# Splits of a cross-network kernel in two groups, half steps as float32r parts, one more z buffer

## The reference

```python
z0 = einsum('bid,bjd->bdij', x0, x0)          # 39 x 39 products, symmetric
cur0 = relu(z0 @ W0)                          # 1521 -> 128
next_h, direct0 = split(cur0, 2)              # 64 and 64
z1 = einsum('bid,bjd->bdij', x0, next_h)      # 39 x 64 products
cur1 = relu(z1 @ W1)                          # 2496 -> 128
z = sum([direct0, cur1], over d)              # 192 values a sample
h = relu(concat(z, dense_ctx) @ W_top1 + b_top1)
y = relu(h @ W_top2 + b_top2) @ W_top3
```

## Time and profile before

| | |
|---|---|
| median of 3 runs | 1515.13 us (1511.45 to 1517.09) |
| the profiled execution | 1511.94 us, its span 1510.1 us |
| PE (TensorE matmuls) busy | 1434.6 us (95%) |
| VectorE (DVE) busy | 1393.3 us (92%) |
| GpSimd (POOL) busy | 939.0 us (62%) |
| ScalarE (ACT) busy | 825.2 us (55%) |
| DMA | 293.08 MB, mean 194 GB/s |

### The profile page before, as it was taken

The page is one execution under the profiler, slowest core; times in us unless marked ns, Lnnn a source line. Parts: engine busy times, 40 slices in busy tenths (PEclk is TensorE's granted clock), DMA queues, the critical chain, the costliest instruction groups (busy, mean ns, idle before and its releaser), DMA issues.

```text
span 1510.1 us, 15015 instructions
## 1 busy us (share of the span) xinstructions
PE 1434.6 (95%) x4458; PEld 794.5 (53%) x4458; DVE 1393.3 (92%) x1253; ACT 825.2 (55%) x897; POOL 939.0 (62%) x604
## 2 busy tenths in 40 slices
PE   3179999999999999999999999999999999999999
PEld 2145555555555555555555555555555555555556
DVE  2179999999999999999999999999999999999993
ACT  0155555655655555655655555655655555655555
POOL 7638888868687786868687786868687780000000
PEclk7589999999999999999999999999999999999999
DMA  5069989999989899999989999899998998898510
GB/s 150 6 160 203 227 216 218 206 220 212 221 198 222 206 217 214 208 223 201 220 203 216 214 212 220 208 213 203 212 216 223 212 210 216 204 222 207 170 35 1
DMA packets 137289, 293.08 MB, mean 194 GB/s; under 512 B 37646, under 2 KB 62878, under 8 KB 137080
## 3 DMA queue, kind: packets, MB, share of 16 engines
q1 hardware_dynamic: 102642, 278.48, 77.2%
q0 software_dynamic: 19200, 4.95, 2.9%
q10 hardware_dynamic: 15366, 8.70, 2.1%
HBM read 284.08 MB, written 7.87 MB: 193 GB/s over the span
## 4 chain that ended last, share of the span: by engine, by line
PE 90%; DVE 4%; issue 2%; another core or an unknown queue 2%; ACT 0%; DMA 0%; DVEq 0%; SPq 0%
PE psB L493 42%; PE psA L493 14%; PE psB L511 7%; PE psB L514 6%; PE psB L518 6%; PE psA L501 2%; PE psA L511 2%; PE psA L514 2%; PE psA L518 2%; PE psB L501 2%; DVE z L902 1%; PE psA L485 1%; DVE z_lo L911 1%; DVE z_split L902 1%
## 5 line engine op out<-in xcount | busy, mean ns | idle before, releaser
L472 POOL DMA_INDIRECT emb<-in_tbl,ids_all x600 | 938.8, 1565 | 309.7 <-issue 178.9
L493 PE MATMUL psB<-z,w 128*128 128x512 f32 x1544 | 690.1, 593 | 5.3 <-DVE z L902 5.3
L767 ACT ACTIVATE z_hi<-z_split 128x1024 fp32r<-128x1024 f32 (+1 forms) x286 | 301.4, 1057 | 464.9 <-DVE z_split L902 372.4
L493 PEld LDWEIGHTS psB<-z,w 128*128 128x128 f32 x1544 | 292.4, 190 | 362.7 <-issue 346.0
L902 DVE TENSOR_TENSOR z<-h_quad,x_lay 128x1024 f32<-128x1024 f32 x354 | 420.5, 1218 | 7.4 <-PE psB L493 5.4
L911 DVE TENSOR_TENSOR z_lo<-z_split,z_hi 128x1024 fp32r<-128x1024 f32 (+1 forms) x286 | 349.3, 1221 | 6.3 <-ACT z_hi L767 3.2
L902 DVE TENSOR_TENSOR z_split<-h_quad,x_lay 128x1024 f32<-128x1024 f32 x222 | 268.4, 1221 | 0.0
L720 ACT ACTIVATE h_quad<-psA 32x1024 f32<-32x1024 f32 x248 | 251.7, 1015 | 6.1 <-DVE feat_side L987 2.4
L493 PE MATMUL psA<-z,w 126*128 126x512 f32 x512 | 241.9, 594 | 0.0
L511 PE MATMUL psB<-z_hi,w_hi 128*128 128x512 f32 x444 | 157.7, 436 | 0.0
L493 PEld LDWEIGHTS psA<-z,w 126*128 126x128 f32 x512 | 97.3, 190 | 98.4 <-issue 92.7
(11 more groups left out here) (113 smaller groups left out, 862.5 us busy)
## 6 DMA issues: line engine op xcount, KB each, us to landing
x_lay<-x_rows SPq DMA_DIRECT2D x1152, 128.0 KB
x_more<-x_rows SPq DMA_DIRECT2D x62, 504.0 KB
bases<-x_rows SPq DMA_DIRECT2D x62, 468.0 KB
x_lay<-x_rows SPq DMA_DIRECT2D x64, 256.0 KB
x_ring<-x_rows SPq DMA_DIRECT2D x31, 504.0 KB
emb<-in_tbl,ids_all POOLq DMA_INDIRECT x600
x_last<-x_rows SPq DMA_DIRECT2D x64, 128.0 KB
x_rows<-x_side ACTq DMA_DIRECT2D x58, 120.0 KB
```

What stands on the lines that cost most here:

```text
L472: nc.gpsimd.indirect_dma_start(emb[t % 2][:, f * D:(f + 1) * D], None, tables[f], bass.IndirectOffsetOnAxis(ids_all[:, t, f:f + 1], 0)).th ...
L493: mm = nc.tensor.matmul(ps[:, cs], w[0:k, :], z[WHOLE_NO[place] % NZ][0:k, cs], start=first, stop=last)
L767: nc.scalar.activation(z_hi[n % NS][0:k, 0:cols], z_split[n % NS][0:k, 0:cols], ACT.Copy).then_inc(z_hi_made, 1)
```

## The change

```diff
-SPLIT0 = (1, 4)
+SPLIT0 = (1, 5, STEPS0 - 1)
 HALF1 = 12
-SPLIT1 = (2, 3, 7, 8, 9, 13, 14)
+SPLIT1 = (2, 3, 4, 9, 10, 11, HALF1)
-EARLY = (2, 3)
+EARLY = (2, 3, 4)
-AFTER = (0, 1, 3, 5, 7, 9, 11)
+AFTER = (0, 1, 4, 5, 7, 9, 11)
 FIRST_AFTER = (1, 3, 4, 5, 7, 9, 11)
-NZ = 4
+NZ = 5
 NS = 3
...
-            def half_product(ps, place, w, last):
-
-                pe.wait_ge(z_made, place + 1)
-                for n in range(2):
-                    rows = slice(n * HROWS, (n + 1) * HROWS)
-                    mm = nc.tensor.matmul(ps[:, n * BANK:(n + 1) * BANK], w[rows, :],
-                                          z[WHOLE_NO[place] % NZ][rows, 0:BANK], start=False, stop=last)
-                mm.then_inc(z_used, 1)
+            def half_product(ps, place, w_hi, w_lo, last):
+
+                n = SPLIT_NO[place]
+
+                def both(w, z, last):
+                    for c in range(2):
+                        rows = slice(c * HROWS, (c + 1) * HROWS)
+                        mm = nc.tensor.matmul(ps[:, c * BANK:(c + 1) * BANK], w[rows, :], z[rows, 0:BANK], start=False, stop=last)
+                    return mm
+
+                pe.wait_ge(z_hi_made, n + 1)
+                both(w_hi, z_hi[n % NS], False)
+                both(w_lo, z_hi[n % NS], False)
+                pe.wait_ge(z_lo_made, n + 1)
+                both(w_hi, z_lo[n % NS], last).then_inc(z_used, 1)
...
                 if s == STEPS0 - 1:
-                    half_product(half(psA, u), at0(u, s), w0[:, ORDER0.index(s), :], True)
+                    n = SPLIT0.index(s)
+                    half_product(half(psA, u), at0(u, s), w0_hi[:, n, :], w0_lo[:, n, :], True)
...
                 if s == HALF1:
-                    half_product(half(psB, u), at1(u, s), w1[:, WHOLE1.index(s), :], False)
+                    n = SPLIT1.index(s)
+                    half_product(half(psB, u), at1(u, s), w1_hi[:, n, :], w1_lo[:, n, :], False)
...
             keep_x(1)
+            high(at0(0, SPLIT0[2]))
             relu0(0)
...
-                    low_before(at1(u, s))
+                    if u or s:
+                        low_before(at1(u, s))
...
+            low(at0(0, STEPS0 - 1))
             dve.wait_ge(z_used, at0(0, STEPS0 - 1) + 1)
```

## The result

The changed kernel takes 1562.25 us (median of 4 runs, 1560.68 to 1563.96) against 1516.11 us for the kernel before beside it: a ratio of 1.0295, 95% interval 1.0242 to 1.0349. The forecast was 1555 us, slower, range 1545 to 1578. The profiled execution after took 1560.68 us, its span is 1558.8 us, 48.7 us more than before; the sum said 40.3.

What follows compares the result with a forecast made beforehand. The prediction took PE to be the bound, VectorE just ahead with about 1% to spare. PE's work +0.3, the stall +39.4 and unit 1's longer issue +0.6 gave +40.3 us on the 1515 us median: 1555, range 1545 to 1578.

Steps and rivals of the forecast that it cites:

- The stall at s=4: ScalarE issues keep_x's two stores ahead of high(s=4), so PE loses 1.36 us in each of 29 units, 39.4 us.
- The z_lo of s=12: VectorE's low part in the second group, ready some 0.1 us before PE wants it; costed at nothing, at most 9 us.
- Unit 1: Besides the stall of 1.36 us, the longer first store issue (up to 1.46 us instead of 0.86) adds 0.6 us.
- PE's own work: Whole steps for splits +11.2 us, float32r half steps side by side with the same edges -10.9 us: +0.3 us in all.
- The 2.1 us of the earlier trace: Read from the profile before as PE's wait for z_lo, from 230 to 1430 us.
- The signs: z_hi of s=4 3.1 us behind the turn, PE idle about 1.0 us before s=4, units 43.8 us, VectorE about 90%.
- Weights are loaded behind the running matmul: Rival: weight loads not hidden in the half steps, 0.11 us at five of six pairs, +18 us, 1573 us; 8%.
- The halves don't run one after another: Rival: the two halves of the half steps run one after another, +44 us on the forecast, 1599 us; 4%.
- the edges didn't vanish: Rival "faster": no stall, and the half steps' edges (0.39 us a unit) vanish, 1503 us; 3%.
- VectorE is not the bound: Rival: VectorE bounds the second group, z_lo of s=12 late by 0.5 us in each unit, +15 us, 1570 us; 9%.
- the prediction's figure of 0.9 us in hand: VectorE's work unchanged by the change, keeping some 0.9 us a unit in hand.
- The clock did fall: Rival: the granted clock falls behind PE's gaps, once a unit, +43 us, 1598 us; 3%.

Runs made afterwards that it cites:

- the fourth experiment: Changed kernel with only keep_x's two stores issued behind high(s=4), the wait for the turn and the copy staying ahead: 1516.92 us, 1.0030 of before.
- the seventh experiment: Kernel of the fourth experiment, with VectorE making the z_lo of s=12 before the product of s=13 instead of behind it: 1475.47 us, 1.0000 of before.
- the eighth experiment: Kernel before the change, its order kept, with its half step s=12 alone as float32r high and low parts and NZ = 5: 1485.10 us, 1.0063 of before.
- the third experiment: Changed kernel with NZ = 4, the fifth z buffer undone: 1570.37 us, 1.0383 of before.
- the second experiment: Kernel before the change, with keep_x one step earlier in ScalarE's body, ahead of the high part of s=3: 1639.94 us in one run, before 1513.44.

## Why the prediction was right, point by point

*The stall at s=4* was the term that decided, and it is shown from both sides: taken out of the changed kernel by moving keep_x, its stores alone, or the turn, and put into the kernel before by one step of ScalarE's order. Its times behind the turn were forecast as 3.13 (z_hi starts), 4.19 (z_hi ends) and 5.46 us (PE's third product), and measured 3.11, 4.17 and 5.48. It costs 1.51 us a unit (44.18 - 42.67 of the fourth experiment) where 1.36 were reckoned. The missing 0.15 us: the prediction ended its count at the start of the third product, but behind a wait PE's first pair takes 0.57 or 0.58 us, not 0.46, and the third product is such a pair (741.28 to 741.86). That gives 0.12 us; the pair behind the first wait is as long, but ends before z_lo is there and costs nothing. The load of the weights starts together with such a pair (740.02, 741.28) and not 0.22 us ahead of it, as it does where pairs follow each other; that this is the cause is likely, but only argued. 29 x 0.15 = 4.4 us.

*The z_lo of s=12* was the term "too close to call", costed at nothing with 0.3 us a unit as its bound. It is 0.19 us (42.67 to 42.48 in the seventh experiment), some 6 us over 31 units. Both terms were sized too small, and the stated range of 1545 to 1578 us had room for them: the mechanism was right, and the forecast was 7 us below the measured 1562.25.

The turns account for the whole. From the turn in unit 2 to that in unit 29 there are 1193.22 us (205.21 to 1398.43) where there were 1147.41 (202.22 to 1349.63): 45.8 us, 27 units by 1.70, which is 1.51 + 0.19. Unit 1 took 46.9 us instead of 44.2, +2.7 where 2.0 were forecast, and the last stall falls behind the last turn, +1.5. These are 50.0 us, and the span grew by 48.7. The start, up to the turn in unit 1, is 0.3 us longer (158.31 against 158.03). Behind the last turn 1.6 us come back: in the trace before, PE waits 0.61 us for a z_lo in unit 31 and 1.06 us for VectorE in the dense network, and in the trace after 0.06 and 0.11.

*PE's own work is unchanged:* +0.3 us was the sum, and the seventh experiment, with PE waiting nowhere, has units of 42.48 us, the same as before. The half steps run side by side, six pairs, 0.23 us apart from the second on: from 658.18, where the split before them is over, to 659.86, and 0.1 us by which the whole passes behind them are longer (10 take 4.56 us, by the rows of 4 and 8 passes they would take 4.46), 1.78 us, where the fp32 pair held PE for 2.11 us. Three pairs for two passes in each, edges as before: 1.77 was forecast.

*A row that was read too wide.* The 2.1 us of the earlier trace rows are waits of the weight loading (PEld), not of PE; PE itself has no wait in that stretch. Nothing in the sum rests on it.

*The signs.* z_hi of s=4 starts 3.11 us behind the turn; PE stands still in front of s=4 in 29 units, 1 to 29, for 0.87 to 0.94 us from unit 2 on; VectorE's busy share went from 92% to 89%, where about 90 was said; units are 44.18 us, where 43.8 was said.

*The rivals.* Weights are loaded behind the running matmul in the 64-row form too: in the seventh experiment the loads of the third pair run from 658.61 to 658.80, while the second pair (658.60 to 659.00) occupies both halves of the rows, and the third starts at 658.84. So the row-group rule of the Trainium skill ("TensorE: Matmul & The Clock Gate", "The mechanism") doesn't bear out here. The halves don't run one after another, and the edges didn't vanish: 1.78 us are 0.40 more than six pairs of 0.23. VectorE is not the bound in the changed kernel; it became so in the eighth experiment, which the prediction's figure of 0.9 us in hand would not have told. The clock did fall in one of the units, unit 1, behind gaps of 0.61 and 1.12 us:

```profile
161.91 0.73 PE L525 MATMUL psB<-z_lo,w_hi 128*128 128x512 f32 x2 [0.61 <-DVE z_lo L921]
163.77 0.73 PE L518 MATMUL psB<-z_hi,w_hi 128*128 128x512 f32 x2 [1.12 <-ACT z_hi L776]
```

```profile
165.00:169.00 4.00, 4.00 (x8) 2.22 (x8) 4.00 (x4) 0.00 (x0) 3.39 (x3) 0.61 0.87 256
```

0.39 x 4 = 1.6 us. In the later units, with 0.87 us and a shorter one, it stayed at 1.00. In the third experiment unit 1 has gaps of the same lengths, 0.62 and 1.12 us, and there it stayed at 1.00 from 162 to 175 us, and the unit took 45.8 us, not 46.9. So the 0.7 us by which unit 1 went beyond its forecast hang on a fall of the clock that gaps of these lengths don't always bring. The rival was given 3%; in the second experiment, with a gap of 2.23 us, it came true in 20 units of 29.

## What to carry to other kernels

When a step becomes one that needs an extra engine's result, look at what stands in that engine's order right ahead of it, DMA issues included, and count from what starts it: here 1.75 us of issuing two stores, harmless ahead of an instruction with time to spare, cost 3%. If such a chain begins at the bottleneck engine's own instruction, a buffer more doesn't shorten it (the stall at s=4 was the same with four and with five); reorder, or start it earlier. And count an engine's reserve in the fullest unit, not as a mean: here 0.95 us on the mean were 0.40 in three units of four, and what the fourth had over went in part in a wait for another engine.

## What was not expected of the hardware

PE's first float32r pair after a wait takes 0.1 us more, at a wait of 0.13 us (half pair before the next step: 716.70 to 717.14, against 659.53 to 659.86) as at one of 0.87 (740.02 to 740.59, 0.57 instead of 0.46). Gaps of 2.2 us and more, one in each of 29 units, brought the granted clock down in 20 of them (to 0.72 on the mean of six us where it was read) and left it at 1.00 in nine, among them one with 2.54 us. Units with the fall are mostly 46.6 to 47.1 us long, those without 46.05 to 46.35, where the kernel before has 42.5. A gap of 0.87 us with a shorter one behind it never did so in 28 units; gaps of 0.6 and 1.12 us close together did in one trace and not in another.
